# Two expert layers in products of rounded halves, and a shorter way to the taps of a state-space convolution

## What is computed

```python
# layer 0: a state-space convolution with 32 heads, its kernel ("taps") from few parameters
dt  = exp(log_dt);  A = -exp(log_A_real) + 1j * A_imag;  dtA = A * dt[:, None]
Cs  = Cc * (exp(dtA) - 1.0) / A
K   = 2.0 * einsum('hn,hnl->hl', Cs, exp(dtA[:, :, None] * arange(512))).real
y   = causal convolution of the masked x with K, plus u * D
# an expert layer (both layers have one): base product, top 2 of 8 experts, rank 16 each
result  = einsum('bnd,od->bno', x, W_base) + b_base
route_w = weights of the top 2 of softmax(x @ W_gate.T), renormalised
h       = einsum('bnd,erd->bner', x, A) * route_w[..., None]
out     = result + einsum('bner,eor->bno', h, B) * SCALING
# between them: attention over a paged cache of keys and values, 32 query heads, 8 key heads
x = x + expert0(conv(x));  x = x + expert1(attention(x))
```

## Time and profile before

| what | us |
|---|---|
| median of 3 runs (2569.38 to 2571.18) | 2570.73 |
| the profiled execution in all | 2569.72 |
| its span, first to last instruction | 2567.9 |
| TensorE busy in the span | 2476.3 (96%) |
| VectorE busy | 1844.1 (72%) |
| ScalarE busy | 1300.9 (51%) |
| GpSimd busy | 723.7 (28%) |
| prologue, about | 0 to 103 |
| expert layer 0, TensorE's products | 103.4 to 210.9 |
| expert layer 1, TensorE's products | 2451.6 to 2562.5 |

### The profile page before, as it was taken

The page is one execution under the profiler, slowest core; times in us unless marked ns, Lnnn a source line. Parts: engine busy times, 40 slices in busy tenths (PEclk is TensorE's granted clock), DMA queues, the critical chain, the costliest instruction groups (busy, mean ns, idle before and its releaser), DMA issues. The chain is left out here.

```text
span 2567.9 us, 53568 instructions
## 1 busy us (share of the span) xinstructions
PE 2476.3 (96%) x15952; PEld 2144.9 (84%) x15952; DVE 1844.1 (72%) x3252; ACT 1300.9 (51%) x3721; POOL 723.7 (28%) x713
## 2 busy tenths in 40 slices
PE   4998999999989799999999999999999989999999
PEld 4645887777868799999999999999999977777733
DVE  7335999999980488888878878788888856666511
ACT  2113555555542477777777777777777731111100
POOL 0032666666650222222222222222222212213000
PEclk7999999999989899999999999999999999999999
DMA  7721333233335589888888988888888886665412
GB/s 292 253 79 56 95 111 97 94 94 94 114 99 168 173 296 304 277 307 284 301 291 285 307 279 306 284 296 299 281 305 286 294 257 210 211 214 195 131 58 74
DMA packets 434115, 542.40 MB, mean 211 GB/s; under 512 B 36980, under 2 KB 350100, under 8 KB 429460
## 3 DMA queue, kind: packets, MB, share of 16 engines
q1 hardware_dynamic: 391012, 394.37, 46.0%
q0 software_dynamic: 36864, 134.23, 16.0%
q10 hardware_dynamic: 6192, 13.19, 1.5%
HBM read 440.65 MB, written 101.01 MB: 211 GB/s over the span
## 5 line engine op out<-in xcount | busy, mean ns | idle before, releaser
L1069 PE MATMUL ps<-at_pt,at_v_raw 128*128 128x128 f32 x4096 | 541.3, 275 | 0.0
L1123 DVE CUSTOM_DVE_ANT_0 at_sm<-ps,at_mask 128x544 f32<-128x544 f32 x512 | 370.0, 723 | 238.4 <-PE ps L1036 231.1
L1069 PEld LDWEIGHTS ps<-at_pt,at_v_raw 128*128 128x128 f32 x4096 | 497.9, 192 | 0.1
L1161 ACT ACTIVATE at_pt<-ps 128x512 f32<-128x512 f32 x512 | 304.4, 594 | 295.5 <-PE ps L1045 295.5
L847 POOL TENSOR_TENSOR pr_m<-pr_qn,tb 128x256 f32<-128x256 f32 x320 | 331.7, 1056 | 279.9 <-DVE pr_qn L816 264.7
L1174 ACT ACTIVATE at_pr<-at_sm,at_nm 128x544 f32<-128x544 f32 x512 | 382.8, 748 | 24.3 <-DVE at_nm L1123 20.8
L681 PE MATMUL ps<-pr_hi,xh 128*128 (+1 forms) x768 | 319.4, 416 | 13.2 <-DVE pr_lo L670 8.7
L1116 DVE TENSOR_TENSOR at_k_lo<-shared,at_k_hi 128x1088 fp32r<-128x1088 f32 x256 | 325.9, 1273 | 0.0
L1045 PE MATMUL ps<-constants,at_pr 128*128 128x128 f32 x2048 | 307.6, 273 | 0.0
L999 POOL DMA_INDIRECT at_v_raw<-v_cache,at_idx x256 | 275.3, 1076 | 114.1 <-issue 62.4
L682 PE MATMUL ps<-pr_lo,xh 128*128 (+1 forms) x768 | 304.9, 397 | 0.0
(11 more groups left out here) (198 smaller groups left out, 4283.6 us busy)
## 6 DMA issues: line engine op xcount, KB each, us to landing
shared<-k_t SPq DMA_DIRECT2D x1024, 128.0 KB, 4.7
qk_t<-pr_stage SPq DMA_DIRECT2D x160, 256.0 KB, 2.3
shared<-qk_t SPq DMA_DIRECT2D x64, 512.0 KB, 7.9
o_t<-at_ot SPq DMA_DIRECT2D x64, 512.0 KB
o_raw<-o_t SPq DMA_DIRECT2D x32, 1024.0 KB, 5.8
shared<-ri_d SPq DMA_DIRECT2D x32, 1024.0 KB, 8.1
w_first<-wqkv SPq DMA_DIRECT2D x12, 1024.0 KB, 6.0
s_k_in<-k_cache SPq DMA_DIRECT2D x16, 512.0 KB, 8.0
```

Source lines behind the costliest of these rows:

```text
L1069: last = e.matmul(ps[:, 5 + w, k * P:(k + 1) * P], v_raw[:, q, c, g * D:(g + 1) * D], pt[:, r, c * P:(c + 1) * P], start=(k == 0 and c == ...
L1123: e.tensor_tensor_reduce(out=halves(sm[:, r, :]), in0=ps[:, 2 * r:2 * r + 2, 0:W], in1=halves(mask[:, q, :]), scale=-SC, scalar=3e38, op0= ...
L1161: e.activation(pt[:, r, :], ps_w, ACT.Copy).then_inc(s_pt, 1)
```

## The change

In both expert layers the A product and the base product are formed from rounded halves instead of float32. ScalarE rounds the activations (`x_hi`), VectorE subtracts (`x_lo`), both while the gate is computed; GpSimd rounds and subtracts a and w. The A product waits for all of a's halves and the block's `x_lo`, the first base product for all of w's halves. `room` is gone; its contents go to `ta` or `shared` (the gate's copy) and into the raw w, which is free by then. In layer 0 `x_hi` and `x_lo` are `xh` and `xl`, written over later by the block's result. In the prologue log_dt and log_a have a semaphore of their own, on which VectorE's chain starts, and the other three loads are waited for ahead of the product with `ai`. The taps products go through the head pairs once, with the two row halves in turn, and VectorE copies bank 1 while ScalarE copies bank 0. Two raw buffers of the output projection are released before the last layer.

```diff
-                e.dma_start(log_dt[:, :], src).then_inc(s_in, 16)
-                e.dma_start(raw[:, 1, :], dram["log_a"]).then_inc(s_in, 16)
+                e.dma_start(log_dt[:, :], src).then_inc(s_dt, 16)
+                e.dma_start(raw[:, 1, :], dram["log_a"]).then_inc(s_dt, 16)
...
-                e.wait_ge(s_in, 16 * 5)
+                e.wait_ge(s_dt, 16 * 2)
...
+                e.wait_ge(s_in, 16 * 3)
                 v(lambda e: e.tensor_tensor(dai, ai[:, :], ex[:, 0, :], ALU.mult))
...
+                e.wait_ge(s_k, 1)
+                e.tensor_copy(kev[:, :, 1, :], ps[0:16, 1, :].rearrange("a (i b) -> a i b", b=32)).then_inc(s_kv, 1)
                 e.wait_ge(s_kv, 2)
...
-                for half in range(2):
-                    e.activation(kev[:, :, half, :], ps[0:16, half, :].rearrange("a (i b) -> a i b", b=32),
-                                 ACT.Copy).then_inc(s_kv, 1)
+                e.activation(kev[:, :, 0, :], ps[0:16, 0, :].rearrange("a (i b) -> a i b", b=32), ACT.Copy).then_inc(s_kv, 1)
...
-                for half in range(2):
-                    rows = slice(half * NS, (half + 1) * NS)
-                    for i in range(HP):
-                        out = ps[0:16, half, i * 32:(i + 1) * 32]
-                        e.matmul(out, ur[rows, i, :], er[rows, i, 0:32], start=True, stop=False)
-                        last = e.matmul(out, ui[rows, i, :], ei[rows, i, 0:32], start=False, stop=True)
+                for i in range(HP):
+                    for a, b, first in ((ur, er, True), (ui, ei, False)):
+                        for half in range(2):
+                            rows = slice(half * NS, (half + 1) * NS)
+                            last = e.matmul(ps[0:16, half, i * 32:(i + 1) * 32], a[rows, i, :], b[rows, i, 0:32],
+                                            start=first, stop=not first)
...
+                for i in range(NB):
+                    for k in range(KB):
+                        cols = slice(i * 512, (i + 1) * 512)
+                        e.wait_ge(s_xh, i * KB + k + 1)
+                        e.tensor_tensor(x_lo[:, k, cols], act[:, k, cols], x_hi[:, k, cols].bitcast(F32),
+                                        ALU.subtract).then_inc(s_xl, 1)
                 e.wait_ge(s_lg, 1)
...
+            @block.gpsimd
+            def _(e):
+                e.wait_ge(s_in, 16 * 4)
+                for k in range(KB):
+                    e.tensor_copy(a_hi[:, k, :], a[:, k, :]).then_inc(s_ah, 1)
+                for k in range(KB):
+                    e.wait_ge(s_ah, k + 1)
+                    e.tensor_tensor(a_lo[:, k, :], a[:, k, :], a_hi[:, k, :].bitcast(F32), ALU.subtract).then_inc(s_al, 1)
+                for k in range(KB):
+                    e.tensor_copy(w_hi[:, k, :], w[:, k, :]).then_inc(s_wh, 1)
+                    e.wait_ge(s_wh, k + 1)
+                    e.tensor_tensor(w_lo[:, k, :], w[:, k, :], w_hi[:, k, :].bitcast(F32), ALU.subtract).then_inc(s_wl, 1)
...
                 for i in range(NB):
+                    for k in range(KB):
+                        cols = slice(i * 512, (i + 1) * 512)
+                        e.activation(x_hi[:, k, cols], act[:, k, cols], ACT.Copy).then_inc(s_xh, 1)
                     e.wait_ge(s_lt, i + 1)
...
                 e.wait_ge(s_in, 16 * 4)
+                e.wait_ge(s_al, KB)
...
+                    e.wait_ge(s_xl, (i + 1) * KB)
                     for k in range(KB):
-                        last = e.matmul(ps[:, 6, :], a[:, k, :], act[:, k, cols], start=(k == 0), stop=(k == KB - 1))
+                        e.matmul(ps[:, 6, :], a_hi[:, k, :], x_hi[:, k, cols], start=(k == 0), stop=False)
+                        e.matmul(ps[:, 6, :], a_hi[:, k, :], x_lo[:, k, cols], start=False, stop=False)
+                        last = e.matmul(ps[:, 6, :], a_lo[:, k, :], x_hi[:, k, cols], start=False, stop=(k == KB - 1))
                     last.then_inc(s_h, 1)
+                    if i == 0:
+                        e.wait_ge(s_wl, KB)
...
                         for k in range(KB):
-                            e.matmul(ps[:, 1 + ob, :], w[:, k, ob * P:(ob + 1) * P], act[:, k, cols],
-                                     start=(k == 0), stop=False)
+                            e.matmul(out, w_hi[:, k, rows], x_hi[:, k, cols], start=(k == 0), stop=False)
+                            e.matmul(out, w_hi[:, k, rows], x_lo[:, k, cols], start=False, stop=False)
+                            e.matmul(out, w_lo[:, k, rows], x_hi[:, k, cols], start=False, stop=False)
```

More of the change, by code:

```diff
@@ L176, in prologue @@
         f, t = (room[:, n * 8:(n + 1) * 8, :].rearrange("p a (b h) -> p (a b) h", h=H) for n in range(2))
-        s_in, s_cst, s_x, s_len, s_v, s_sin, s_u, s_k, s_kv, s_ev, s_out, s_kt, s_kc, s_mm, s_y, s_rope = (
-            sem(n) for n in ("in", "cst", "x", "len", "v", "sin", "u", "k", "kv", "ev", "out", "kt", "kc", "mm", "y", "rope"))
+        s_dt, s_in, s_cst, s_x, s_len, s_v, s_sin, s_u, s_k, s_kv, s_ev, s_out, s_kt, s_kc, s_mm, s_y, s_rope = (
+            sem(n) for n in ("dt", "in", "cst", "x", "len", "v", "sin", "u", "k", "kv", "ev", "out", "kt", "kc", "mm", "y", "rope"))
         s_ki, s_ko = ([sem(f"{n}{q}") for q in range(TB)] for n in ("ki", "ko"))
@@ L423, in load, with ffn @@
         e.dma_start(self.lb[:, :], dram[lb_n]).then_inc(self.s_in, 16)
-def ffn(nc, ps, dram, inputs, tag, act, src, out, scaling, cst, halves=None, tables=None, ahead=None):
+def ffn(nc, ps, dram, inputs, tag, act, src, out, scaling, cst, lgt, halves=None, tables=None, ahead=None):
     NB = T // 512
@@ L436, in ffn @@
         w, a, g, lb, bias, s_g, s_in = (inputs.w, inputs.a, inputs.g, inputs.lb, inputs.bias, inputs.s_g, inputs.s_in)
+        w_hi, w_lo = (sb(n, [P, KB, L], F32R) for n in ("w_hi", "w_lo"))
+        a_hi, a_lo = (sb(n, [P, KB, E * R], F32R) for n in ("a_hi", "a_lo"))
+        x_hi, x_lo = halves if halves else (sb(n, [P, KB, T], F32R) for n in ("x_hi", "x_lo"))
         resid = sb("resid", [P, 2, KB, 512])
@@ L440, in ffn @@
         route = sb("route", [P, NT, E])
[L441 to L446, removed]
+        route_t, wexp, hw = w[0:E, 0:2, :], w[:, 2, :], w[:, 3, :]
+        s_xh, s_xl, s_ah, s_al, s_wh, s_wl, s_lt, s_lc, s_lg, s_v, s_e2, s_rt, s_rte, s_we, s_wx, s_h, s_hw, s_mm, s_ev, s_hi, s_lo, s_tab = (
+            sem(n) for n in ("xh", "xl", "ah", "al", "wh", "wl", "lt", "lc", "lg", "v", "e2", "rt", "rte", "we", "wx", "h", "hw", "mm", "ev",
                              "hi", "lo", "tab"))
@@ L531, in _ @@
                                             halves[0][:, ob, cols].bitcast(F32), ALU.subtract).then_inc(s_lo, 1)
-            if tables:
-                @block.gpsimd
-                def _(e):
+            @block.gpsimd
[10 more added lines that the diff above has]
+                    e.tensor_tensor(w_lo[:, k, :], w[:, k, :], w_hi[:, k, :].bitcast(F32), ALU.subtract).then_inc(s_wl, 1)
+                if tables:
                     e.wait_ge(s_nw, 32)
@@ L597, in _ @@
                         wait(e, s_ev, (i - 1) * KB + ob + 1)
+                        rows, out = slice(ob * P, (ob + 1) * P), ps[:, 1 + ob, :]
                         for k in range(KB):
-                            e.matmul(ps[:, 1 + ob, :], w[:, k, ob * P:(ob + 1) * P], act[:, k, cols],
-                                     start=(k == 0), stop=False)
+                            e.matmul(out, w_hi[:, k, rows], x_hi[:, k, cols], start=(k == 0), stop=False)
+                            e.matmul(out, w_hi[:, k, rows], x_lo[:, k, cols], start=False, stop=False)
+                            e.matmul(out, w_lo[:, k, rows], x_hi[:, k, cols], start=False, stop=False)
                     if i == 0:
@@ L1358, in build @@
                 ffn(nc, ps, dram, first_in, "0", y_t, dram["x_t"], x1_t, 1.0, cst,
-                    halves=(xh, xl), tables=(cos, sin, ta, tb),
+                    ta[0:E, 0:T // D, :].rearrange("p a d -> p (a d)"), halves=(xh, xl), tables=(cos, sin, ta, tb),
                     ahead=(w_first[0][:, :, :], dram["wqkv"][0:1, :, :].rearrange("o (k p) n -> p (o k) n", p=P), w_first[1]))
@@ L1362, in build @@
         with ExitStack() as last:
-            w_raw = last.enter_context(nc.sbuf_tensor("w_raw", [P, REP, L], F32, side="right"))
-            o_raw = last.enter_context(nc.sbuf_tensor("o_raw", [P, 2, 512 // S, P], F32, side="right"))
+            raw = last.enter_context(ExitStack())
+            w_raw = raw.enter_context(nc.sbuf_tensor("w_raw", [P, REP, L], F32, side="right"))
+            o_raw = raw.enter_context(nc.sbuf_tensor("o_raw", [P, 2, 512 // S, P], F32, side="right"))
             ri_b = shared[:, 0:2 * 512 // S * P].rearrange("p (q x) -> p q x", q=2)
@@ L1371, in build @@
             output_projection(nc, ps, dram, o_t, ri_d, att, results, second_in)
-            ffn(nc, ps, dram, second_in, "1", att, x1_t, out_t, 2.0, cst)
+            raw.close()
```

(1 more changed line is left out.)

## The result

The changed kernel takes 2543.05 us (median of 4 runs, 2539.14 to 2543.54) where the kernel before took 2570.95 us (median of 4); the ratio is 0.9889, 95% interval 0.9872 to 0.9906, so 1.1% less. The forecast was 2546 us, range 2540 to 2553. The profiled execution is the fastest of the four, 2539.14 us with a span of 2537.3 us; against the profile of before that is 30.6 us, some 3 us more than the medians differ by.

The account below looks back on a forecast made before the run. TensorE, or what feeds it, bounds the expert layers and prologue. Gains of 5.35 (prologue), 7.15 (layer 0) and 11.85 us (layer 1) sum to 24.35 us, giving a forecast of 2546 us, range 2540 to 2553.

Parts of the forecast that it names:

- The gain per product: Expert layers: three rounded matmuls of 0.2366 us replace a float32 product, saving 0.148 us each, 11.85 us a layer.
- What runs beside: Expert layers: ScalarE's roundings and VectorE's subtractions hidden under the gate; route chain pushed at most some 6 us, also hidden.
- The stall in layer 0: Before layer 0's first base product: TensorE waits 3.0 us for GpSimd's low halves of w, bounds none and 4.4 us.
- The clock: Layer 0, after the stall: TensorE's granted clock falls once, costing 1.7 us, bounds 0 and 2.
- The prologue: Before the first expert layer: 2.3 + 3.3 + 0.45 - 0.7 = 5.35 us gained.
- the guess from the two length loads: Prologue start: log_a lands at about 5.9 us, judged by loads of 4.7 and 6.0 us; gain 2.3 us.
- The row halves: Prologue taps products: alternating row halves run side by side, 6.7 us become 3.4; gain taken 3.3 us.
- The wait between the taps' write and the load: Prologue: earlier taps' write and Toeplitz loads meet DMA engines busy with key pages; 0.7 us lost, bounds 0 and 2.
- Rival A: Layer 0: GpSimd slips between VectorE's subtractions, neither stall nor clock loss; 4.7 us less, 2542 us; chance 0.18.
- Rival B: Prologue taps: row halves not side by side in steady stream; 3.3 us more, 2550 us; chance 0.14 with its companion.
- C: Expert layers: exclusion costs more, full 4.4 us in layer 0, a few in layer 1; 2551 us; chance 0.12.
- D: Expert layers: products of halves lose full clock; up to 114 us more, 2660 us; chance 0.03 including the unseen.

Follow-up runs that it names:

- x_right: Changed kernel with layer 1's x_hi and x_lo placed at the other end of on-chip memory; layer 1 took 105.0 us against 102.0.
- low_late: Changed kernel with VectorE's subtractions for blocks 1 to 3 behind the route chain, rope tables behind them; 2537.75 us in one run.
- after_beside: Changed kernel unaltered, timed again on another chip; 2605.1 us beside 2634.5 us of the kernel before, ratio 0.9889.
- no_alternate: Changed kernel with taps products one row half after the other; products 6.8 us instead of 3.6, first Toeplitz product 2.65 us later.
- all_five: Changed kernel with VectorE's chain waiting for all five loads again; taps products 2.6 us later, first Toeplitz product 1.7 us later.
- copies_act: Changed kernel with both taps copies on ScalarE; addition of D at 44.17 instead of 43.93 us, first Toeplitz product 50.20 against 50.27 us.
- after_again: Changed kernel unaltered, timed again in more rounds; 2598.6 us beside 2629.7 us of the kernel before, ratio 0.9886.

## Why the prediction was right

**The gain per product.** The step from the earlier trace rows held in its kind and was too small. The matmuls of halves start 0.2345 us apart in layer 0, as in the output projection less 1%, but 0.2268 us in layer 1 (0.2366 in the sum). Layer 1 gave 14.0 us instead of 11.85; sixty matmuls per block at 0.2268 instead of 0.2366 are 0.59 us, 2.35 us in four blocks. This is a term that was mis-sized, and `x_right` takes it back to 0.2343 us with the move of x_hi and x_lo.

**What runs beside.** ScalarE's and VectorE's parts were hidden. The route ended 5 us after the first base product began and was wanted 6 us after that.

**The stall in layer 0.** Forecast 3.0 us, found 0.6 us, in other traces of the same kernel up to 2.2. The exclusion is real (`low_late`), and GpSimd did interleave with VectorE, but it took 15.2 us where I had 17.6. I had charged ten GpSimd operations with a whole subtraction of 0.68 us each, 6.8 us; what the rows of after show is twelve operations that are longer, by 0.46 us for a rounding of w (1.07 instead of 0.61), 0.32 us for a subtraction of w (1.60 instead of 1.28) and some 0.45 us for one of a (0.90 instead of 0.45), 4.9 us in all. The likely reason is that a part of VectorE's instruction is already over when GpSimd's wait begins; no run shows it apart. The step that failed is the charge of ten subtractions in full. The other half of the wait, when GpSimd starts, came out as forecast (14.7 us ahead of TensorE's demand, 14.6 in the sum), and is what varies between traces: the landing of lb decides it.

**The clock.** I charged one fall of 1.7 us in layer 0, behind the stall. There was one of that size, at another place (the low-rank products); in `after_beside` there were two, one of them where I had put it. That the profiled layer had just one is luck: traces of the changed kernel show 5.40 us and 3.70 us for the same eight matmuls of layer 0 behind the same gap. Layer 0 gave 10.0 us instead of 7.15; 2.4 us of the difference is the shorter stall, the rest the distance of starts.

**The prologue.** Forecast 5.35 us, found 5.7 at the first Toeplitz product and 6.0 at the gate. The load of log_a landed so that the chain gained 2.6 us (forecast 2.3); the guess from the two length loads was good. An estimate by the fixed cost of about 2.0 us that the Trainium skill gives ("DMA: Bandwidth & Descriptors", section "Anatomy of one DMA — SWDGE (gpsimd) path"; the section is on loads issued by GpSimd, and SyncE issued these) would have had the chain start near 3.6 us. It started at 5.68 us, so this trace does not agree. The row halves gave 3.2 us (forecast 3.3, `no_alternate`): groups of four starts stand at the distance of 0.11 us that groups of two had. The Trainium skill ("TensorE: Matmul & The Clock Gate", section "Measured speedup vs the span model") gives 3.07 times for four row tiles, 77% of four; an estimate by that share, 1.53 times for two, is not what happened: 6.8 us became 3.3 to 3.65. The wait between the taps' write and the load, longer beside busy DMA engines, took 0.6 us (forecast 0.7, `all_five`); that it was so near is partly luck, since the nine traces with the early write have 0.05 to 1.3 us. The copies gave 0.38 us up to the addition of D (forecast 0.45, `copies_act`). And 0.3 us came from a clock that returned a little earlier, which is chance.

**Sum.** 24.35 us forecast, 30.6 us in the profiled execution, 27.9 us between the medians. The errors of the profiled execution go the same way: 2.4 us for the stall, 2.15 for layer 1 and 0.4 for layer 0 by the distance of starts, 0.65 for the prologue, and 0.6 for the stages between, which I had let move as a block. The medians differ by 2.7 us less than the profiled executions do; in which stage the three other runs lost it no trace shows. Rival A came nearest to what happened in layer 0. Rival B is refuted by `no_alternate`, C by the wait of 0.5 to 2.2 us in layer 0 and none in layer 1, and D by the granted clock of 1.00 in the base products, with the one stretch of 0.60 in `after_beside` as all that was seen of it.

## What to carry to other kernels

A float32 product is worth splitting in halves where TensorE is the chain and the splitting is hidden behind other work, and its gain is read from a stretch of the same kernel that already does it, by the distance of starts. Two engines that exclude each other cost less here than the sum of their instructions, but move the one without a deadline behind the one with one: here that freed 5 us of GpSimd. Behind a block of products look for the small dependent steps that could have been done among them; closing 2.3 us once per layer, with the falls of the clock that went with it, gave 6.5 us, and the whole prologue 4.7.

## What was not expected of the hardware

The same form of matmul starts every 0.2268 us or every 0.2343 us when only the place of tiles on chip differs (`after_beside` and `x_right`, same chip). A gap of 1.6 us before the same products is followed by a fall of the granted clock in some traces and not in others (5.40 or 3.70 us), and a pause of 2.8 us before layer 1's gate by 15.60 or 13.91 us. The small taps products, 32 columns each, took 3.5 us at a granted clock of 1.00 (`after_again`) and 3.65 us at 0.50 (`after_beside`). Chips differ by 58 to 63 us in the attention stage, whatever the kernel, and hardly in layer 1: 102.3, 102.2 and 102.0 us for the changed kernel on three of them.
